# Moving x's norm, beta, the router and the weight pieces to other stages in a fused attention and feed-forward kernel on one core

## The reference, cut to what matters

```
xn  = layernorm(x)                                   # over the 1024
q, k = ws(wq) y + bq, ws(wk) y + bk ;  v = ws(wv) xn + bv        # ws: rows of the weight normalised
S   = softmax(q k^T / scale)  per head (8 heads of 32)
o   = ws(wo) (S v) + bo + xn ;  o = norm over the 256 channels, * gamma + beta
x   = x + tanh(g_xattn) * o
h   = silu(silu(layernorm(x) w1^T) w3^T) w2^T        # 4096 rows of 1024
out = x,  and gates (top 2 of 8 by softmax(rows wr^T)) * h summed into rows 0 to 7
```

## Time and profile before

| | before |
|---|---|
| median of three runs | 1135.68 us |
| the profiled execution: its time / its span | 1137.7 us / 1135.8 us |
| mean granted TensorE clock, share of full speed | 0.974 |
| busy in the span: PE, DVE, ACT, POOL | 1043.5, 805.0, 469.9, 415.6 us |
| instructions: PE, DVE, ACT, POOL | 6502, 1915, 714, 498 |

### The profile page before, as it was taken

The page is one execution under the profiler, slowest core; times in us unless marked ns, Lnnn a source line. Parts: engine busy times, 40 slices in busy tenths (PEclk is TensorE's granted clock), DMA queues, the critical chain, the costliest instruction groups (busy, mean ns, idle before and its releaser), DMA issues.

```text
span 1135.8 us, 17656 instructions
## 1 busy us (share of the span) xinstructions
PE 1043.5 (92%) x6502; PEld 594.8 (52%) x6502; DVE 805.0 (71%) x1915; ACT 469.9 (41%) x714; POOL 415.6 (37%) x498
## 2 busy tenths in 40 slices
PE   4672898999999999999999999999999999999998
PEld 2461454645555455645555455645555455644452
DVE  5987688975798668975798668975798668963221
ACT  4378344263335424263335424263336424262341
POOL 2493015831267014831267014831167015820000
PEclk9786889999999999999999999999999999999999
DMA  8705983153002700153002600162002600063000
GB/s 306 193 20 107 217 205 46 38 147 114 1 20 87 191 0 0 37 149 109 0 18 92 185 0 0 37 157 101 0 18 97 181 0 0 0 166 132 1 1 2
DMA packets 129377, 90.20 MB, mean 79 GB/s; under 512 B 103135, under 2 KB 112933, under 8 KB 129341
## 3 DMA queue, kind: packets, MB, share of 16 engines
q1 hardware_dynamic: 127280, 88.16, 28.1%
q10 hardware_dynamic: 2060, 1.58, 0.5%
HBM read 47.75 MB, written 16.81 MB: 57 GB/s over the span
## 4 chain that ended last, share of the span: by engine, by line
PE 55%; DVE 21%; POOL 9%; ACT 6%; issue 6%; DMA 2%; SPq 1%; POOLq 0%; ACTq 0%; DVEq 0%
PE bank L665 39%; PE bank L539 6%; DVE ub L1227 5%; POOL xbuf L415 3%; POOL mtmp L412 3%; POOL coc L376 2%; DVE ub L1247 2%; PE bank L548 2%; DVE bst L1176 2%; DVE ub L1243 2%; ACT ub L864 2%; PE bank L612 1%; ACT h_hi L905 1%; DVE x_hi L1187 1%; DVE act_t L1344 1%
## 5 line engine op out<-in xcount | busy, mean ns | idle before, releaser
L665 PE MATMUL bank<-xt_hi,w1b 128*128 128x512 f16 x1024 | 326.4, 381 | 1.8 <-DMA xt_lo<-mrow 1.2
L665 PE MATMUL bank<-w3b,h_hi 128*128 128x512 f16 x1024 | 304.5, 379 | 0.0
L665 PE MATMUL bank<-xt_lo,w1b 128*128 128x512 f16 x512 | 194.9, 381 | 0.0
L665 PE MATMUL bank<-w3b,h_lo 128*128 128x512 f16 x512 | 194.0, 379 | 0.0
L899 ACT ACTIVATE act_t<-bank,fs 128x512 f32<-128x512 f32 x128 | 86.9, 679 | 191.3 <-PE bank L665 191.3
L1349 DVE SCALAR_TENSOR_TENSOR h_lo<-act_t,h_hi 128x512 f16<-128x512 f32 x128 | 98.8, 772 | 91.7 <-ACT h_hi L905 91.7
L665 PEld LDWEIGHTS bank<-xt_hi,w1b 128*128 128x128 f16 x1024 | 100.5, 98 | 116.9 <-issue 3.7
L905 ACT ACTIVATE h_hi<-act_t 128x512 f16<-128x512 f32 x128 | 80.8, 631 | 193.8 <-DVE act_t L1344 193.8
L1344 DVE SCALAR_TENSOR_TENSOR act_t<-act_t,bank 128x512 f32<-128x512 f32 x128 | 86.6, 676 | 100.6 <-ACT act_t L899 100.3
L665 PEld LDWEIGHTS bank<-w3b,h_hi 128*128 128x128 f16 x1024 | 98.0, 98 | 76.0
L432 POOL TENSOR_TENSOR ub<-bo_b,mcur 128x512 f32<-128x512 f32 x64 | 65.4, 1051 | 189.7 <-DVE dg L1202 176.9
(11 more groups left out here) (197 smaller groups left out, 1792.8 us busy)
## 6 DMA issues: line engine op xcount, KB each, us to landing
xbuf<-in_x_dram SPq DMA_DIRECT2D x16, 1024.0 KB, 8.7
out_dram<-xbuf SPq DMA_DIRECT2D x16, 1024.0 KB, 4.4
x_lo<-in_ctx_dram SPq DMA_DIRECT2D x16, 512.0 KB, 3.4
mrow<-in_mask_dram SPq DMA_DIRECT2D x16, 512.0 KB, 4.5
w1b<-in_w_dram SPq DMA_DIRECT2D x8, 512.0 KB, 6.7
w3b<-in_w_dram SPq DMA_DIRECT2D x8, 512.0 KB, 7.8
xbuf<-in_w_dram SPq DMA_DIRECT2D x1, 4096.0 KB, 13.7
xt_hi<-x_hi SPq DMA_TRANSPOSE x32, 3.4
```

The lines of the kernel that those rows point to most:

```text
L665: mm = pe.matmul(bk[:, :], left, right, start=d == 0 and n == 0, stop=d == FT - 1 and n == 2)
```

## The change

x's norm: `ln1` on DVE moves to stages 1 and 2 and its coefficients on POOL to 2 and 3, with two sets of coefficients instead of one; ACT's `normed` now writes both the f16 copy and the f32 form, four instructions instead of two, behind `ffn` at stage 1 for b = 0 and ahead of `t1_high` at stage 4 for b = 1; `x_high` is gone on DVE (and on ACT in the prologue). On POOL, `bias_part` and `x_low` come at stages 2 and 3, behind waits for `s_ready`. `add_beta` waits for `ub_ready` of b = 1, the end of DVE's `bias_tiles`, at stage 6. The router's three steps move from groups 1, 2, 3 to 4, 5, 6. In pass 0 the weight pieces are split behind `ffn`, mostly two to a group, in another order of slots, and x of pair 1 is loaded from ACT's queue in group 0 instead of SP's. DVE splits the softmax of b = 1 around `t1_low`. POOL multiplies one more pair of numbers behind each maximum of y. PE waits for a turned w3 piece only where it is used.

```diff
@@ -57,7 +57,7 @@
-ROUTER = (1, 2, 3)
+ROUTER = (4, 5, 6)
@@ -82,12 +82,12 @@
     def w_slot(i):
-        return ((3, 0), (4, 0), (0, 0), (1, 0), (2, 0), (0, 1), (1, 1), (2, 1),
-                (0, 2), (1, 2), (2, 2), (0, 3), (1, 3), (2, 3), (0, 4), (0, 5))[i]
+        return ((3, 0), (4, 0), (0, 0), (1, 0), (2, 0), (4, 1), (0, 1), (1, 1),
+                (2, 1), (0, 2), (1, 2), (0, 3), (2, 2), (0, 4), (2, 3), (0, 5))[i]
     def w_blocks(g):
-        return {0: (5, 6, 7), 1: (8, 9), 2: (10, 11), 3: (12, 13), 4: (14,), 6: (15,)}.get(g, ())
+        return {0: (6,), 1: (7, 8), 2: (9, 10), 3: (11, 12), 4: (13, 14), 5: (15,)}.get(g, ())
@@ -164,7 +164,7 @@
-        co = sb("co", [P, 4, 2])
+        co = sb("co", [P, 2, 4, 2])
@@ -182,7 +182,7 @@
-        pspare = sb("pspare", [P, 1])
+        pspare = sb("pspare", [P, 2])
@@ -213,7 +213,7 @@
-            mcur_set ln1_stat ln1_mv ln1_var ln1_rstd ln1_coef xs_ready xhi_ready xlo_ready mtmp_step xpre_ready
+            mcur_set ln1_stat ln1_mv ln1_var ln1_rstd ln1_coef xs_ready xlo_ready mtmp_step xpre_ready
@@ -295,10 +295,11 @@
             def pair(j, last=False):
-                load_x(j)
+                else:
+                    load_x(j)
@@ -383,14 +384,15 @@
-                pool.tensor_tensor(pspare[:, :], minus[:, 0:1], minus[:, 0:1], ALU.mult)
+                pool.tensor_tensor(pspare[:, 0:1], minus[:, 0:1], minus[:, 0:1], ALU.mult)
-            def ln1(q):
-                coefs(q, mv, co, CH, EPS, XS, "ln1", (sm["xs_ready"], q))
+                pool.tensor_tensor(pspare[:, 1:2], minus[:, 0:1], minus[:, 0:1], ALU.mult)
+
+            def ln1(q, b):
+                coefs(q, mv, co[:, b], CH, EPS, XS, "ln1", (sm["xs_ready"], q - 1))
             def x_low(q, b):
-                pool.wait_ge(sm["xhi_ready"], q + 1)
+                pool.wait_ge(sm["xs_ready"], q + 1)
@@ -436,29 +438,35 @@
-                if s in (3, 4):
-                    ln1(2 * j + s - 3)
-                if s in (2, 3):
-                    bias_part(2 * j + s - 2, s - 2)
-                if s in (5, 6):
-                    x_low(2 * j + s - 5, s - 5)
-                if s == 7:
+                if s == 2:
+                    pool.wait_ge(sm["s_ready"], 2 * j + 1)
+                    ln1(2 * j, 0)
+                    bias_part(2 * j, 0)
+                    x_low(2 * j, 0)
+                if s == 3:
+                    ln1(2 * j + 1, 1)
+                    pool.wait_ge(sm["s_ready"], 2 * j + 2)
+                    bias_part(2 * j + 1, 1)
+                    x_low(2 * j + 1, 1)
+                if s == 6:
+                    pool.wait_ge(sm["ub_ready"], 2 * j + 2)
                     add_beta(j, 0, 0)
-                    values(2 * j, 0)
+                if s == 7:
+                    values(2 * j, 0)
+                    add_beta(j, 1, 1)
-                    add_beta(j, 1, 1)
-            ln1(0)
+            ln1(0, 0)
             x_low(0, 0)
-            ln1(1)
+            ln1(1, 1)
@@ -654,9 +662,9 @@
-                    if g == FT and d == 0 and first_pair(j):
-                        for slot, n in enumerate((6, 4, 4)):
-                            pe.wait_ge(w_turned[slot], 32 * n)
+                    if g == FT and first_pair(j):
+                        slot, used = w_slot(FT + d)
+                        pe.wait_ge(w_turned[slot], 32 * (used + 1))
@@ -787,12 +795,16 @@
         def _(act):
-            def normed(q, b, c_, s_coef, s_done):
-                act.wait_ge(s_coef, q + 1)
+            def normed(q, b):
+
+                act.wait_ge(sm["ln1_coef"], q + 1)
+                if isinstance(q, int) and q < 2:
+                    act.wait_ge(sm["qk_mm"], CT * (q + 1))
                 for c in range(CH):
-                    ins = act.activation(xs[b][:, c, :], xa[b][:, c, :], ACT.Identity,
-                                         bias=c_[:, 3, c:c + 1], scale=c_[:, 2, c:c + 1])
-                ins.then_inc(s_done, 1)
+                    for x in (x_hi[:, b], xs[b]):
+                        ins = act.activation(x[:, c, :], xa[b][:, c, :], ACT.Identity, bias=co[:, b, 3, c:c + 1],
+                                             scale=co[:, b, 2, c:c + 1])
+                ins.then_inc(sm["xs_ready"], 1)
@@ -875,12 +887,15 @@
+                if s == 3:
+                    t1_high(2 * j)
-                if s in (3, 4):
-                    t1_high(2 * j + s - 3)
+                if s == 4:
+                    normed(2 * j + 1, 1)
+                    t1_high(2 * j + 1)
@@ -890,8 +905,8 @@
-                if s in (4, 5):
-                    normed(2 * j + s - 4, s - 4, co, sm["ln1_coef"], sm["xs_ready"])
+                if s == 1:
+                    normed(2 * j, 0)
@@ -913,18 +928,28 @@
-                    for i in w_blocks(g):
-                        w_high(i)
-                        act.wait_ge(w_turned[(3, 4, 1, 2, 0)[n]], (32, 32, 128, 128, 192)[n])
+                        act.wait_ge(w_turned[(3, 4, 1, 2, 0)[n]], (32, 64, 96, 128, 192)[n])
+                if w3:
+                    if g == 0:
+                        load_next_x()
+                    for i in w_blocks(g):
+                        w_high(i)
+            def load_next_x():
+
+                for b in range(2):
+                    act.wait_ge(out_done[b], 16)
+                    act.wait_ge(sm["xs2_ready"], CH * (1 + b))
+                    act.dma_start(xa[b], xd[2 + b]).then_inc(x_in[b], 16)
@@ -939,12 +964,6 @@
-            def x_high(b):
-
-                act.wait_ge(sm["qk_mm"], CT * (b + 1))
-                act.wait_ge(sm["xs_ready"], b + 1)
-                act.activation(x_hi[:, b], xs[b], ACT.Copy).then_inc(sm["xhi_ready"], 1)
@@ -966,13 +985,11 @@
-            normed(0, 0, co, sm["ln1_coef"], sm["xs_ready"])
-            x_high(0)
+            normed(0, 0)
-            normed(1, 1, co, sm["ln1_coef"], sm["xs_ready"])
             t1_high(1, bk=rbk)
-            x_high(1)
+            normed(1, 1)
@@ -989,6 +1006,7 @@
+            w_high(5)
@@ -1181,10 +1199,6 @@
-            def x_high(q, b):
-                dve.wait_ge(sm["xs_ready"], q + 1)
-                dve.tensor_copy(x_hi[:, b], xs[b]).then_inc(sm["xhi_ready"], 1)
@@ -1308,16 +1322,20 @@
-                if s in (1, 3):
-                    softmax(2 * j + s // 2, s // 2)
+                if s == 1:
+                    softmax(2 * j, 0)
+                if s == 3:
+                    below_largest(2 * j + 1, 1)
+                    t1_low(2 * j)
+                    block_weights(2 * j + 1, 1)
+                if s in (1, 2):
+                    ln1(j, s - 1)
-                if s in (3, 4):
-                    t1_low(2 * j + s - 3)
-                    ln1(j, s - 3)
+                if s == 4:
+                    t1_low(2 * j + 1)
-                    x_high(2 * j + s - 5, s - 5)
@@ -1401,10 +1419,10 @@
+                ffn(j, g)
-                ffn(j, g)
@@ -1497,6 +1515,7 @@
+            w_low(5)

```

## The result

The kernel after takes 1112.07 us (median of four runs, 1110.56 to 1113.95), the kernel before beside it 1136.08 (1135.35 to 1136.77): a ratio of 0.9789, 95% interval 0.9777 to 0.980. That is 24 us less, twice the 12.4 forecast: inside the stated range, but outside the forecast's own 1117 to 1129 and at the time of rival B. The profiled execution took 1113.95 us, its span is 1112.2.

A forecast was written before the change was run, and what follows sets the result against it. PE's own work was taken as the floor, busy 124.2 of 127.5 us a pass; 9.6 us from six passes plus 2.8 from pass 0 and the prologue made 12.4 off, giving 1123 us, range 1110 to 1134.

The forecast's parts named there:

- rival B: Steady passes: DVE meets POOL nowhere, so all 3.1 to 3.2 us of waits go; 1109 to 1116 us, chance 0.20.
- the three waits: PE's waits in each steady pass: 0.84 us for x_low, 1.24 for DVE at the fifth piece, 1.1 for ACT.
- x_low and the fifth piece, of 2.1 us: PE's waits in the long product, for POOL's x_low and DVE's attention_out: 0.6 us of 2.1 won a pass.
- ACT, of 1.1 us: Wait of the transposes of b = 1 for ACT: 1.0 us won a pass, bounds 0.3 and 1.1.
- The mis-sized term: DVE's h_lo of groups 5 and 7 and top_two, stretched beside POOL's work: 0.5, 0.9 and 0.7 us, sum 2.1.
- the middle: Start of attention_out and PE's fifth piece: 0.6 us won, between 2.1 won and 1.1 lost.
- Rival C: DVE waits out whole pieces of POOL's work; steady passes gain 0.3 us at most; about 1134 us, chance 0.14.
- Rival D: Stage 2 of every pass: ACT's normed delays scores of b = 1; 1148 us at a 2.5 us delay, chance 0.08.
- The third wait: Transposes of b = 1 wait 1.1 us for ACT, which waits for POOL's coefficients; 1.0 us to be won a pass.
- the sign named for it: If the forecast is right, the coefficients of b = 1 on POOL would be seen waiting for DVE; no size given.
- Pass 0 and the prologue: First pass and what precedes it: 3.5 us won in pass 0, 0.7 lost in the prologue, net 2.8 us.
- The first wait for q: Pass 0, score product: wait falls from 3.3 to 1 us, some 4.5 us won; the second grows from 2.1 to about 4.

The follow-up runs named there:

- e8: Kernel after, with three small POOL products (about 0.8 us) ahead of add_beta, behind its wait: 1112.90 us, ratio 0.9793 to the kernel before.
- e7: Kernel after, without POOL's two waits for the end of the softmax ahead of bias_part: 1118.21 us, ratio 0.9844 to the kernel before.
- e6: Kernel after, with the router's three steps back in groups 1, 2, 3: 1115.63 us, ratio 0.9822 to the kernel before.
- e9: Kernel before, with x's low part left out, POOL writing zeros in its place: 1108.08 us, ratio 0.9753 to the kernel before.
- e1: Kernel after, with add_beta no longer waiting for the end of bias_tiles: 1175.48 us, ratio 1.0344 to the kernel before.
- e13: Kernel after, without POOL's second small product behind each maximum of y: 1154.57 us, ratio 1.0164 to the kernel before.
- e4: Kernel after, with ACT's normed of b = 0 behind q_scaled of b = 1 in pass 0 alone: 1115.96 us, ratio 0.9814 to the kernel before.
- e10: Kernel after, with pass 0's weight pieces, load of x and PE's single w3 wait as in the kernel before: 1120.58 us, ratio 0.9861 to it.
- e11: Kernel after, with the router's steps in groups 3, 4, 5: 1136.53 us, ratio 1.0002 to the kernel before.
- e12: Kernel after, router in groups 3, 4, 5; in pass 0, normed and the weight pieces of groups 2 and 3 moved later: 1139.59 us, ratio 1.0032 to before.

## Why the prediction was right, and where it was off

**The bound and the waits.** PE's floor and the three waits were the right place to look: 18.7 of the 23.6 us came from there. By terms, for one pass:

| term | forecast | measured |
|---|---|---|
| x_low and the fifth piece, of 2.1 us | 0.6 | 1.6 (0.46 left) |
| ACT, of 1.1 us | 1.0 | 1.1 |
| PE's own busy time | 0 | 0.5 |
| sum, and with short gaps | 1.6 | 3.3 |

That the time lies in the range all the same is no merit of the sum: the range took in most of B, and the mechanism forecast gives half of the gain.

**The mis-sized term** is the 2.1 us by which POOL would stretch DVE's work: 0.5 for h_lo of group 5, 0.7 in `top_two`, 0.9 for h_lo of group 7. They measured 0.17, 0.70 and 0, in all 0.87. The neighbours met as foretold (x_low ran from 428.29 to 433.2, h_lo and `top_two` lay in it, beta began beside h_lo of group 7), so rival B's mechanism is false though its time is right. The overruns of the earlier trace rows were taken over as if a meeting had a fixed price; e8, e7 and e6 show that it costs what is left of POOL's instruction, 0.1 to 0.8 us for the same pair. By that rule the prediction's own starts (x_low from 436.7, h_lo of group 5 at 439.8) give about 0.15 for h_lo of group 5, an estimate, and not 0.5; the 0.7 in `top_two` was met by accident, since it was taken from another neighbourhood. `attention_out` came 5.7 us behind PE's first piece; the sum had 4.7 for no meeting and 6.8 for the middle.

**The second omission** is PE's busy time: 124.23 was taken as a floor, but each stall adds to it. The last matmul ahead of a stall counts as busy to its own end (0.38 us, where otherwise the next one starts after 0.22), and the first behind it can be longer (0.44 for 0.38 in the earlier trace rows). Three stalls are gone: that for x_low (0.22 of busy time), that for ACT (0.06), and one of 0.03 us ahead of `out_times_scores` at 433.61 in the kernel before (0.24). Together that makes the 0.5 by which 123.72 is less; e9, with almost no wait, has 123.79.

**Rival C** (whole pieces) is what happens where the two engines run long rows of instructions against each other: in e1 seven of eight tiles each let one of POOL's pass. What keeps the kernel out of it is the new wait of `add_beta`. **Rival D** did not come: q was scaled by 412.47 against scores at 412.92, the slack of 0.4 us that the prediction had. It hung on something that I had costed at nothing in its place, the product behind the maximum, which was hidden as foretold, but hides with it the 7 us of idle POOL that e13 shows. **The third wait** went, but the sign named for it did not come: the coefficients of b = 1 did not wait for DVE. The statistics were there at 468.23, while POOL was in `add_beta` until 468.6 (its last product, of 1.27 us, began at 467.37), and the coefficients followed at 468.60 without idle time. Nor was h_lo of group 7 longer than 0.69.

**Pass 0 and the prologue** were put at 2.8 and gave 4.9: PE's first w1 product came 1.8 us later (116.84 against 115.08; forecast 0.7), and pass 0 behind it took 6.7 us less (forecast 3.5). The first wait for q went altogether, the second is 4.2 (forecast 4). For its cause I named `normed` and two pieces on ACT; by e4 that is wrong in part, DVE's `ln1` and its two pieces come first. And the new order of the pieces, with PE's finer wait for w3, is worth more than the 3.5 us forecast: 8.5 by e10, with the other parts of the change in place. What the single moves (the casts, the norm's statistics, the softmax split) are worth by themselves, no run here shows.

## What to carry to other kernels

When a wait is costed from rows in which two engines slow each other, look up at what point of the other's instruction each began: what one pays is the remainder, from nothing to a whole instruction, and long rows of short instructions pay it every time. So a late but solitary place for GpSimd's work can be worth more than an early one. And an instruction that looks idle may decide where a longer idle time falls: before a small instruction is costed at nothing, see what the idle time ahead of it is, and where that would go without it.

## What I had not expected of the hardware

- POOL stood idle 5.65 to 6.36 us ahead of each maximum of the kernel after, and in e13 7.0 to 8.0 us ahead of the next ordinary instruction, behind the waits of passes 1 to 5. There this adds to the wait in full; a product of 0.18 us moved it into idle time, worth 42 us.
- A row of DVE instructions of 0.41 us ran in step with POOL's of 1.04 and 1.27 us, at 1.18 us each, with POOL nearly undisturbed: the loss is on the side of the shorter instructions.
- POOL's writing of zeros (four pieces, 1.92 us, from 433.61 and from 440.31 in e9) lay beside the h_lo of 435.11 and of 441.40, and both took 0.69 us.
- A stall of 2.02 us of PE had two sequels: in e11 the mean granted clock was 0.65 for the next 4.8 us; in e12, behind the same wait for cb at the same place of the pass, it stayed at 1.00.
